# Keys and receptances of the next chunk ahead of the later outputs in a recurrence on one Trainium2 core

## The reference

```python
r = xr @ Wr
k = xk @ Wk
v = xv @ Wv
g = jax.nn.silu(xg @ Wg)
w = jnp.exp(-jnp.exp(ww))
def step(state, rkvw):
    r_t, k_t, v_t, w_t = rkvw
    a = k_t[..., :, None] * v_t[..., None, :]
    y = jnp.einsum('bhk,bhkv->bhv', r_t, state + u[None, :, :, None] * a)
    new_state = w_t[..., :, None] * state + a
    return (new_state, y)
...
yn = (y - mu) * jax.lax.rsqrt(var + EPS)
return yn.reshape(Bb, Tt, Cc) * g @ Wo
```

## Time and profile before

| | us |
|---|---|
| Median of three runs | 1455.2 |
| The runs | 1459.51, 1447.1, 1455.2 |
| Span of the profiled execution | 1357.2 |
| Recurrence in it, first to last matmul | about 557 to 1080 |

### The profile page before, as it was taken

How to read it: one execution, slowest core, us unless ns; L and a number is a source line. 1 busy time by engine, 2 the same in 40 slices (tenths; PEclk the granted TensorE clock), 3 DMA queues, 4 the chain that set the end, 5 groups by cost and what they waited for, 6 DMA issues and landing times. The chain is left out here.

```text
span 1357.2 us, 34954 instructions
## 1 busy us (share of the span) xinstructions
PE 1148.5 (85%) x14041; PEld 820.0 (60%) x14041; DVE 926.0 (68%) x1959; ACT 613.3 (45%) x1310; POOL 551.3 (41%) x537
## 2 busy tenths in 40 slices
PE   7999999976599999478999898898996658999970
PEld 4677777754488888235555555555554437888860
DVE  4778787757765656568678695968756376565646
ACT  2334343313255555144737455474635233555544
POOL 3333333202377776324151432415141115777750
PEclk9999999978699999698999999999999778999995
DMA  8032222108743332200000001000000095333338
GB/s 302 24 126 93 81 90 83 64 1 296 248 169 104 103 105 90 75 31 3 33 3 33 24 12 33 3 33 4 1 3 2 18 389 166 103 104 101 104 101 345
DMA packets 50683, 125.66 MB, mean 93 GB/s; under 512 B 7649, under 2 KB 26977, under 8 KB 47713
## 3 DMA queue, kind: packets, MB, share of 16 engines
q1 hardware_dynamic: 36896, 86.20, 17.7%
q0 software_dynamic: 13632, 37.24, 8.7%
HBM read 79.63 MB, written 43.78 MB: 91 GB/s over the span
## 5 line engine op out<-in xcount | busy, mean ns | idle before, releaser
L1090 POOL DMA_INDIRECT ffn_xs<-xn_rows,ffn_from_row x142 | 137.6, 969 | 123.7 <-DVE ffn_second_y_at L1472 81.0
L1098 POOL DMA_INDIRECT y_rows<-ffn_ys,ffn_to_row x142 | 140.1, 987 | 55.1 <-issue 35.4
L1253 PE MATMUL ffn_ps_h<-ffn_w_high,ffn_xst 128*128 x568 | 155.3, 396 | 0.6 <-issue 0.6
L1500 DVE TENSOR_TENSOR ffn_act_in<-ffn_silu_g,ffn_ps_h 128x256 f32<-128x256 f32 x142 | 59.9, 422 | 139.0 <-ACT ffn_silu_g L1132 139.0
L1132 ACT ACTIVATE ffn_silu_g<-ffn_ps_h 128x256 f32<-128x256 f32 x142 | 54.8, 386 | 144.3 <-PE ffn_ps_h L1253 144.3
L1273 PE MATMUL ffn_ps_o<-ffn_w,ffn_act_t 128*128 x284 | 117.2, 435 | 0.5 <-DVE ffn_act_t L1505 0.5
L1253 PEld LDWEIGHTS ffn_ps_h<-ffn_w_high,ffn_xst 128*128 128x128 f32 x568 | 97.4, 190 | 18.2 <-issue 1.1
L1833 POOL TENSOR_TENSOR rec_mixed_w<-rec_mixed_w,rec_xnt 128x512 f32<-128x512 f32 x16 | 17.2, 1091 | 207.5 <-DVE rec_mixed_w L2634 207.5
L1253 PE MATMUL ffn_ps_h<-ffn_w_low,ffn_xst 128*128 x284 | 89.8, 398 | 0.0
L644 DVE TENSOR_TENSOR ret_probs<-ret_score,ret_causal 128x2048 f32<-128x2048 f32 x32 | 73.3, 2292 | 18.7 <-PE ret_score L485 18.7
L1275 PE MATMUL ffn_ps_o<-ffn_w,ffn_act_t 128*128 x284 | 79.2, 279 | 0.0
(11 more groups left out here) (353 smaller groups left out, 2894.8 us busy)
## 6 DMA issues: line engine op xcount, KB each, us to landing
home<-y_rows SPq DMA_DIRECT2D x30, 512.0 KB, 5.0
w_split<-home SPq DMA_DIRECT2D x24, 512.0 KB, 4.1
ffn_w_high<-w_split SPq DMA_DIRECT2D x8, 1024.0 KB, 8.8
ffn_w_low<-w_split SPq DMA_DIRECT2D x8, 1024.0 KB, 10.7
ffn_w<-w_split SPq DMA_DIRECT2D x8, 1024.0 KB, 14.4
home<-in_f_w SPq DMA_DIRECT2D x12, 512.0 KB, 6.1
xn_rows<-home SPq DMA_DIRECT2D x12, 512.0 KB, 11.7
out<-x SPq DMA_DIRECT2D x8, 512.0 KB, 5.7
```

The costliest lines, as they stand in the source:

```text
L1090: pool.indirect_dma_start(xs[:, n % SLOTS, :], None, xn_rows[:], bass.IndirectOffsetOnAxis(ap=from_row[:, n:n + 1], axis=0)) \
L1098: pool.indirect_dma_start(y_rows[:], bass.IndirectOffsetOnAxis(ap=to_row[:, m:m + 1], axis=0), ys[:, m % SLOTS, :], None).then_inc(ys_stor ...
L1253: mm = pe.matmul(ps_h[:, u % 2, :], one_pass(xst[:, u % 2, part, k, :]), one_pass(w1[w_part][k][:, bass.ds(e, E_COLUMNS)]), start=(part + ...
L1500: dve.tensor_tensor(act_in[:, u % 2, :], silu_g[:, u % 2, :], ps_h[:, u % 2, FF:2 * FF], ALU.mult) \
```

## The change

TensorE: `keys(n + 1)` stands ahead of `outputs(n, 1)`, `receptances(n + 1)` ahead of `outputs(n, 2)` and `outputs(n, 3)`. ScalarE: `k_out(n + 1)` stands behind `decay_of(n + 1)`, ahead of `y_raw(n, 1)`; `r_out(n)` stands ahead of `y_raw(n - 1, 2)`, and waits in addition until the near products are done and until all outputs of the chunk behind are out, since these read the r tile that it overwrites. VectorE: `near_products` read the receptances in PSUM (`even`), and no longer wait for the copy; the first product goes into the tile of the mixed keys (`products_0`), which is free once the keys are out, instead of `y_near`; `near_0` reads that tile; the wait for `r_ready` moves into `to_twos`, that for `y_summed` to `times_v_0`; the last mask stands behind the moments.

```diff
@@ -1659,6 +1659,7 @@
         r_32p = sb("r_32p", [P, KT, HEADS, TC // 64, 32])
 
         y_near = sb("y_near", [P, KT, TC])
+        products_0 = mixed["k"]
         near_1 = sb("near_1", [P, KT, FOURS, 3])
         near_23 = sb("near_23", [P, KT, FOURS, 3])
         v = sb("v", [P, CT, C])
@@ -1950,6 +1951,9 @@
 
                 def r_out(c):
                     act.wait_ge(r_in_psum, c + 1)
+                    act.wait_ge(chain, c * CHAIN + NEAR_1)
+                    if c >= 1:
+                        act.wait_ge(y_in_psum, c * CT)
                     act.activation(r[:], even[:], ACT.Copy).then_inc(r_ready, 1)
 
                 def v_out(c):
@@ -2060,16 +2064,13 @@
 
                 for n in range(-2, CHUNKS + 1):
                     now, ahead, behind = 0 <= n < CHUNKS, 0 <= n + 1 < CHUNKS, n >= 1
-                    if now:
-                        k_out(n)
                     if ahead:
                         norm(n + 1)
+                    if now:
+                        r_out(n)
                     if behind:
                         y_raw(n - 1, 2)
                         y_raw(n - 1, 3)
-                    if now:
-                        r_out(n)
-                    if behind:
                         square_out(n - 1)
                         silu(n - 1, 0)
                         silu(n - 1, 1)
@@ -2114,6 +2115,8 @@
                         y_raw(n, 0)
                     if ahead:
                         decay_of(n + 1)
+                    if ahead:
+                        k_out(n + 1)
                     if now:
                         y_raw(n, 1)
                         act.preload_act_table_set("silu_and_others")
@@ -2258,7 +2261,7 @@
                     else:
                         pe.wait_ge(xnt_ready, min(2, CHUNKS))
                     for kt in range(KT):
-                        mm = pe.matmul(even[:, kt, :], same_head[:], y_near[:, kt, :], start=True, stop=True)
+                        mm = pe.matmul(even[:, kt, :], same_head[:], products_0[:, kt, :], start=True, stop=True)
                     mm.then_inc(near_in_psum, 1)
 
                 def near(c, into, source):
@@ -2473,15 +2476,15 @@
                         scores_by_4(n, 3)
                         scores_by_16(n, 3)
                         scores_by_32(n, 3)
+                    if ahead:
+                        keys(n + 1)
+                    if now:
                         outputs(n, 1)
                     if ahead:
-                        keys(n + 1)
+                        receptances(n + 1)
                     if now:
                         outputs(n, 2)
                         outputs(n, 3)
-                    if ahead:
-                        receptances(n + 1)
-                    if now:
                         gate(n, 0)
                         gate(n, 1)
                     if n + 2 < CHUNKS:
@@ -2507,21 +2510,21 @@
                     step(dve.tensor_tensor(w[2 * n][:].rearrange("p k b -> p (k b)"), pairs[:, :, 0], pairs[:, :, 1], ALU.mult))
 
                 def near_products(c):
-                    dve.wait_ge(r_ready, c + 1)
+                    dve.wait_ge(r_in_psum, c + 1)
                     dve.wait_ge(k_ready, c + 1)
                     if c >= 1:
-                        dve.wait_ge(y_summed, c * KT)
                         dve.wait_ge(near_added, c * 3)
                     for kt in range(KT):
-                        step(dve.scalar_tensor_tensor(y_near[:, kt, :], r[:, kt, :], bonus[:, kt:kt + 1], k[:, kt, :],
+                        step(dve.scalar_tensor_tensor(products_0[:, kt, :], even[:, kt, :], bonus[:, kt:kt + 1], k[:, kt, :],
                                                       ALU.mult, ALU.mult))
-                    step(dve.tensor_tensor(near_1[:].rearrange("p k b i -> p (k b) i"), fours(r)[:, :, 1:4], fours(k)[:, :, 0:3],
+                    step(dve.tensor_tensor(near_1[:].rearrange("p k b i -> p (k b) i"), fours(even)[:, :, 1:4], fours(k)[:, :, 0:3],
                                            ALU.mult))
 
                 def to_twos(c):
                     after(c, NEAR_1)
                     step(dve.tensor_tensor(blocks(k, 1)[:, :, 0, :], blocks(k, 1)[:, :, 0, :], of_blocks(products(1)[:, :, 1], 1),
                                            ALU.mult))
+                    dve.wait_ge(r_ready, c + 1)
                     step(dve.tensor_tensor(blocks(r, 1)[:, :, 1, :], blocks(r, 1)[:, :, 1, :], of_blocks(products(1)[:, :, 0], 1),
                                            ALU.mult))
                     pairs = near_23[:].rearrange("p k b i -> p (k b) i")
@@ -2598,6 +2601,8 @@
                 def times_v_0(c):
                     dve.wait_ge(vt_ready, c + 1)
                     dve.wait_ge(near_in_psum, c * 3 + 1)
+                    if c >= 1:
+                        dve.wait_ge(y_summed, c * KT)
                     dve.tensor_tensor(y_near[:], even[:], vt[:], ALU.mult).then_inc(near_v, 1)
 
                 def times_v_1(c):
@@ -2856,12 +2861,12 @@
                         mix_g(n + 1)
                     if then:
                         stats_of_x(n + 2, 1)
-                    if now:
-                        mask(n, 3)
                     if ahead:
                         decay_product(n + 1, 1)
                     if then:
                         moments_of_x(n + 2)
+                    if now:
+                        mask(n, 3)
                     if behind and n < CHUNKS:
                         stats_of_out(n - 1)
                 dve.wait_ge(x_stats_ready, TILES)
```

## The result

The changed kernel takes 1480.7 us (1479.0 to 1484.3, 4 runs) against 1453.2 (1447.1 to 1459.5, 4 runs) of the kernel before on the same chip: ratio **1.020, 95% interval 1.016 to 1.024**. The forecast, slower, with 1470 as the time, had the sign, and the time lies in the range of 1454 to 1486; but it lies just above the 1463 to 1479 that the forecast's own course of things allowed, near the 1477 of rival C, and the loss is 27 to 30 us where the sum said 15. What has to be found is where the other twelve or more come from.

A forecast was written before the change was run, and what follows sets the result against it. Bound: the chain gate product, SiLU, table load, tokens, token_shift, VectorE's dense work, decays, last scores. Seven changes +18.2, first chunk +1.6, stalls -3.0, expert rows -1.6 sum to +15.2 us: time 1470, range 1454 to 1486.

The forecast's parts named there:

- the forecast's own course of things: Whole kernel slower by the y chain at full clock, 1463 to 1479 us; chance 0.42.
- rival C: TensorE's new standstill ahead of values brings the lower clock in three of seven changes, +7 us more, 1477; chance 0.15.
- Outputs later, near products earlier, PSUM as fast as SBUF: From S, end of last scores: outputs 3 end 11.83, near products start 8.9, end near 11.2, r_out starts 11.97.
- The y chain 2.1 us later in each change: ScalarE and GpSimd: y_raw, sum_y, square and SiLUs queue behind r_out; second SiLU ends 18.2 after last scores, was 16.06.
- Contention 0.5: GpSimd's sum_y beside VectorE's to_twos takes longer: 0.5 us per change, bounds 0 and 1.0.
- The period grows by the same: VectorE waits some 6 us at token_shift for the tokens, so each period grows as much as the second SiLU is late.
- Rival A: Faster: VectorE's chain starts four microseconds earlier, TensorE's waits of 2.3 us a chunk go if tokens don't hold token_shift; 1434; chance 0.08.
- Issue stalls -3.0: TensorE's stalls in outputs 1, together 5.2 us, shrink as long matmuls break up short ones: -3.0, bounds 0 and -5.2.
- Expert rows -1.6: VectorE's one wait of 1.55 us for the next expert rows' load goes, being wanted 2.6 us later: -1.6, bounds 0, -1.6.
- First chunk +1.6: Transposition waits for r_out(0), now behind near_products(0), about 2.4 us later: +1.6, bounds 0 and 2.4.
- The clock: TensorE's clock behind the gap ahead of values; not in the forecast's sum, put only into rival C, +7 us, chance 0.15.

The follow-up runs named there:

- e2: Changed kernel, with VectorE's first operation on the copied receptances also waiting until sum_y is over; ratio 1.015 to the kernel before.
- e6: Kernel before with only TensorE's new order and k_out moved; near products still read the copy, r_out stays behind y_raw; ratio 1.0007.
- e4: Changed kernel with y_raw 2 and 3 put back ahead of r_out on ScalarE; ratio 1.008 to the kernel before.
- e8: e4 with the transposition between the two gate products and the tokens' copy ahead of squares and SiLUs; ratio 1.008 to the kernel before.
- e12: Kernel before with the transposition between the two gate products and the tokens' copy ahead of squares and SiLUs; ratio 1.011.
- e1: Kernel before, run again without any edit for a second profile; ratio 1.001.
- e5: Changed kernel run again as it stands, for a second profile; ratio 1.022 to the kernel before.
- e3: Changed kernel with the second gate product computed twice, same values, inside TensorE's gap ahead of values; ratio 1.018 to the kernel before.
- e7: Kernel before, old order, with only the near products reading receptances in PSUM and r_out waiting for them; ratio 1.009.
- e9: Kernel before with one edit, mask 3 behind the decay product and the moments; ratio 1.000.
- e11: Kernel before with TensorE's new order, k_out moved and the mask edit, without the near products' part; r_out behind y_raw; ratio 1.002.

## Why the prediction was right, and why too small

By its own steps:

- *Outputs later, near products earlier, PSUM as fast as SBUF.* Right to 0.3 us: outputs 3 end at S + 11.57 (11.83), near products start at S + 8.74 (8.9) and end at 11.01 (11.2), `r_out` starts at 11.73 (11.97).
- *The y chain 2.1 us later in each change.* Right in mechanism; without contention it is 18.07 - 16.20 = 1.87 (e2). The order gives 0.88 of it (e6), the copy ahead of y_raw about the rest: e4 takes back 1.49, which is that and half of the contention.
- *Contention 0.5.* Mis-sized: 0.95 (e2), the upper bound. The reason given for half of it, that `to_twos` is over before the second add ends, left out that VectorE's last product is stretched too, from 0.69 to 1.77 us, so that they meet for longer. 3.2 us of the missing twelve.
- *The period grows by the same.* Right in the number, wrong in the chain, and so in part by luck: both chains start at the second SiLU. The text led it through the table load, tokens and `token_shift`; e8 and e12 take that wait out and gain nothing. It goes from the second SiLU straight to values on TensorE. The 0.83 us in the earlier trace rows was the wait of an engine that wasn't the bound. Rival A rested on the same misreading, that freeing `token_shift` would decide: it is free in e6, e8 and e12, and none of them is faster than before.
- *Issue stalls -3.0.* Too small. The gaps in A that the profile calls issue fall by 4.2 between e1 and e5 (6.9 to 2.7) and by 6.4 between the first profiles (9.0 to 2.5). In the changed traces none is left in outputs 1. The sum of A over seven times its smallest value falls by 6.1 between e1 and e5 (9.8 to 3.7), with the 1.7 us that the lower clock adds in e1's fifth A.
- *Expert rows -1.6.* VectorE's wait for them goes in the seven changes (in the first chunk both profiles of the changed kernel have one of 1.2), but most of it lay where VectorE had slack. Behind the wait of 1.55 in the earlier trace rows TensorE waited 0.65 us for `mixed_w`, and that B is 42.47 instead of 41.8 to 42.0; in e1 a wait of 0.85 at the same place leaves B at 41.80. So the term was worth -0.7 at most, not -1.6.
- *First chunk +1.6.* Too small. `r_out(0)` starts 4.55 us after ScalarE was free, behind the near products, and the transposition behind it 3.87 us after TensorE was, where it was 1.21; that is 2.66 more, beyond the upper bound of 2.4:

```profile
646.01 1.02 ACT L1957 ACTIVATE rec_r<-rec_even 128x1024 f32<-128x1024 f32 x1 [4.55 <-DVE rec_near L2520]
647.18 1.22 PE L2137 MATMUL rec_even<-home 128*128 128x128 f32 x8 [3.87 <-ACT rec_r L1957]
```

  The head grows by 4.7 between e1 and e5; the clock is low there for a time in all kernels, and which part is the wait's and which the clock's stays open. The six profiles with a transposition wait of 1.21 have heads from 83.7 to 91.2 (mean 87.3), the eight with 3.87 from 88.3 to 94.8 (mean 90.9).
- *The clock, left out of the sum and given to rival C at 0.15.* This is the step that failed. It was set up as another course of things, at 7 us more and "three of seven changes", and it came beside my own: four of seven, behind the gap that my sum foresaw (2.1 to 2.6, measured 2.94). The four slow values of e5 take 7.9 us more than at full clock, and B grew by 8.8; the rest of that is a balance of stalls and of the last chunk. In no change with a gap of up to 1.9 us ahead of values are they slow; of those with gaps from 1.98 us on, 17 are and 13 aren't. A forecast in which TensorE stands still anew needs a term for the clock in its sum. How much of the time the slow values cost is argued from the traces; e3, which filled the gap, doesn't show it in the time.

So the sum of 15.2 was low by the clock (8.8), the contention (3.2), the first chunk (3.1) and the expert rows (up to 1.6), and high by the y chain (1.6) and the stalls (3.1). With the measured terms: 7 x (1.87 + 0.95) = 19.7, less 6.1, plus 4.7, plus 8.8 is 27.1, against the 27.2 of the pair e1 and e5. The list closes by construction, as the terms are differences of the same two traces; e2, e4, e6 and e7 are what ties them to causes.

What stays open: the head, as said; and when a gap lowers the clock. The near products alone cost 12 us in the timed runs, of which 7 x 1.30 + 2.4 = 11.5 are accounted for, though its trace has 19.8 us more in the recurrence than e1, 10.7 of them in the head. No version found beats the kernel before: the nearest are e6, e9 and e11, all within 0.3%.

## What to carry to other kernels

An instruction that is made to wait takes with it all that stands behind it on its engine. Here a copy that nobody needed sooner was put ahead of the chain that the bounding engine waits for, and its place alone held two thirds of the loss (e4). When the parts of a change measured one by one don't add up, look first for a part that none of them holds. To find which wait bounds, cut the period at two marks and look which part changes; then take the suspected wait out, as e12 did, for two starts that hang on the same event move together and can't be told apart by a table. And a new gap on TensorE is priced with what the clock does behind it.

## What the hardware showed

- A gap of 2.94 us on TensorE between a transposition and the values was followed by the lower clock in four of seven changes, with the same share in two executions, but not in the same changes (0.57 of the full clock over 7 us in the slowest case, +1.6 to +3.0 us each). Behind gaps of 0.85 to 1.87 us ahead of values it was in none, but elsewhere the lower clock did follow shorter gaps: one of 1.22 us ahead of short matmuls in e1, one of 1.59 in e6.
- Where the clock falls at the head differs between executions and moves the profile by more than some edits do. The same work of the third 12 us of the recurrence, ahead of all that the edit changes, has a clock of 0.94 in e1 and e5, and 0.64 in e6, here e5 and e6:

```profile
575.69:587.69 12.00, 8.21 (x23) 3.06 (x23) 5.48 (x17) 4.90 (x8) 5.70 (x7) 0.94 0.00 0
```

```profile
576.61:588.61 12.00, 9.44 (x19) 3.19 (x18) 6.59 (x20) 2.92 (x4) 5.30 (x6) 0.64 0.00 0
```

- A two-input VectorE operation on SBUF of 128x512 beside a GpSimd add takes 1.77 us instead of 0.69 (0.68 in e2), and the two adds of 128x512 take 3.43 instead of 2.48.
- Issue stalls of 0.2 to 1.95 us come in runs of short matmuls on a tile of 64x64 and less; eight matmuls of 128x512 between two runs were enough that none was left in the first of the later outputs.
